# The closing of batch 6 on GpSimd, and the routed rows of batch 7 loaded from ScalarE's queue

## The reference

```python
x = x + ga * attention(h)                      # per batch
h = layernorm(x) * (1 + cb) + sb
topk_w, topk_i = group_limited_topk(softmax(h @ gate_weight.T))   # 2 of 8 experts per token
routed = sum over the 2 chosen experts of  w * (silu(h @ gate) * (h @ up)) @ down
shared = silu(h @ sh_gate.T) * (h @ sh_up.T) @ sh_down.T
x = x + gb * (routed + shared)                 # gb: one row of 256 per batch
```

## Time and profile before

| | |
|---|---|
| median of 3 runs | 278.69 us (278.34 to 280.42) |
| the profiled execution | 280.89 us, its span 278.9 us |
| mean granted clock of TensorE | 0.993 |
| busy: PE, DVE, ACT, POOL | 91%, 73%, 58%, 47% of the span |
| chain that ended last: PE, DVE, issue, ACT | 70%, 12%, 6%, 4% |

### The profile page before, as it was taken

The page is one execution under the profiler, slowest core; times in us unless marked ns, Lnnn a source line. Parts: engine busy times, 40 slices in busy tenths (PEclk is TensorE's granted clock), DMA queues, the critical chain, the costliest instruction groups (busy, mean ns, idle before and its releaser), DMA issues.

```text
span 278.9 us, 6194 instructions
## 1 busy us (share of the span) xinstructions
PE 254.6 (91%) x1797; PEld 235.3 (84%) x1797; DVE 202.8 (73%) x632; ACT 161.4 (58%) x429; POOL 132.1 (47%) x148
## 2 busy tenths in 40 slices
PE   0889999898999999999999889989999999999980
PEld 0787778797989999998979778989999999999960
DVE  1675974147998674388479778466899978989986
ACT  2447558968655754836536375355666666666630
POOL 4120313744255037785895375600455645555650
PEclk9999999999999999999999999999999999999997
DMA  7795007154224102242134023525754367485663
GB/s 230 272 346 160 0 7 228 49 158 125 74 66 127 47 1 98 95 124 86 67 119 139 34 84 123 202 81 130 199 151 129 123 205 235 135 239 211 227 190 118
DMA packets 28175, 37.89 MB, mean 136 GB/s; under 512 B 4476, under 2 KB 20711, under 8 KB 28144
## 3 DMA queue, kind: packets, MB, share of 16 engines
q1 hardware_dynamic: 23648, 28.63, 34.2%
q0 software_dynamic: 3216, 8.46, 8.1%
q10 hardware_dynamic: 1280, 0.41, 0.6%
HBM read 25.18 MB, written 12.71 MB: 136 GB/s over the span
## 4 chain that ended last, share of the span: by engine, by line
PE 70%; DVE 12%; issue 6%; ACT 4%; POOL 2%; DMA 2%; ACTq 1%; DVEq 0%; SPq 0%; POOLq 0%
PE bank L348 15%; PE bank L350 14%; PE bank L349 14%; PE bank L1148 4%; PE bank L1120 3%; PE bank L1367 3%; PE bank L1140 2%; PE bank L1103 2%; PE bank L1131 2%; PE bank L1112 2%; PE bank L1021 1%; PE bank L1398 1%; PE bank L1397 1%; DVE h2T_lo L1442 1%; DMA h2all<-routed_in 1%
## 5 line engine op out<-in xcount | busy, mean ns | idle before, releaser
L1496 POOL DMA_INDIRECT routed_out<-yo_all,dest x35 | 38.6, 1102 | 44.2 <-ACT yo_all L1438 32.1
L711 POOL DMA_INDIRECT routed_in<-h2all,slot_u x32 | 31.6, 986 | 21.8 <-DVE slot_u L692 11.6
L348 PE MATMUL bank<-experts_w,h2T_lo 128*128 x117 | 39.7, 339 | 0.1
L350 PE MATMUL bank<-experts_w,h2T_hi 128*128 x117 | 36.2, 309 | 0.0
L349 PE MATMUL bank<-experts_w,h2T_hi 128*128 x117 | 36.0, 307 | 0.0
L348 PE MATMUL bank<-h2T_hi,wsgu_lo 128*128 128x256 f32 (+1 forms) x96 | 27.9, 290 | 0.7 <-ACT og L482 0.7
L350 PE MATMUL bank<-h2T_hi,wsgu_hi 128*128 128x256 f32 (+1 forms) x96 | 27.0, 281 | 0.0
L349 PE MATMUL bank<-h2T_lo,wsgu_hi 128*128 128x256 f32 (+1 forms) x96 | 26.9, 281 | 0.0
L1422 ACT ACTIVATE wstage<-bank 128x176 f32<-128x176 f32 x39 | 12.4, 318 | 22.1 <-PE bank L350 22.1
L348 PEld LDWEIGHTS bank<-experts_w,h2T_lo 128*128 128x128 f32 x117 | 22.2, 190 | 0.8 <-issue 0.6
L349 PEld LDWEIGHTS bank<-experts_w,h2T_hi 128*128 128x128 f32 x117 | 22.3, 190 | 0.0
(11 more groups left out here) (278 smaller groups left out, 827.8 us busy)
## 6 DMA issues: line engine op xcount, KB each, us to landing
h2all<-routed_in SPq DMA_DIRECT2D x39, 130.0 KB, 2.5
wstage<-gu_t SPq DMA_DIRECT2D x8, 352.0 KB, 3.2
res<-x SPq DMA_DIRECT2D x4, 512.0 KB, 8.9
mx_all<-modrow SPq DMA_DIRECT2D x8, 256.0 KB, 3.2
mh_all<-modrow SPq DMA_DIRECT2D x8, 256.0 KB, 3.4
exchange<-routed_out SPq DMA_DIRECT2D x4, 512.0 KB, 4.8
wmod_s<-w_mod SPq DMA_DIRECT2D x3, 512.0 KB, 10.0
out<-res SPq DMA_DIRECT2D x6, 256.0 KB, 3.1
```

The costliest lines, as they stand in the source:

```text
L348: pe.matmul(out_ap, l[1], r[0], start=start, stop=False)
L350: return pe.matmul(out_ap, l[0], r[0], start=False, stop=stop)
L711: pool.indirect_dma_start(out=routed_in, out_offset=bass.IndirectOffsetOnAxis(slot_u[:, i, j:j + 1], 0), in_=h2all[:, j % (2 * NB), :], in ...
L1496: pool.indirect_dma_start(out=routed_out, out_offset=bass.IndirectOffsetOnAxis(dest[:, t % 16:t % 16 + 1], 0), in_=yo[t % 6], in_offset=No ...
```

## The change

Batch 6 joins batch 5 in BY_POOL: its three closing steps run on POOL behind those of batch 5, and not on DVE. FIN_AT gets a fifteenth number (37), so that batch 4 "out" is taken at tile step 37 of DVE. `load_rows` of batch 7 goes from SP, where it stood behind that of batch 6, to ACT, where it stands in tile step 37 between the copy L1426 of that tile and the copy out (L1434) of tile 36.

```diff
-            BY_POOL = (5,)
+            BY_POOL = (5, 6)
...
-                    for b in (6, 7):
-                        load_rows(sp, b)
+                    load_rows(sp, 6)
                     store(sp, 4)
                     store(sp, 6)
                     store_half(sp, 7, 0)
...
                         act_tile_act(act, t, r)
+                        if t == LASTT - 1:
+                            load_rows(act, B - 1)
...
-                    FIN_AT = (20, 21, 22, 23, 24, 25, 28, 29, 30, 31, 32, 33, 35, 36)
+                    FIN_AT = (20, 21, 22, 23, 24, 25, 28, 29, 30, 31, 32, 33, 35, 36, 37)
```

## The result

The changed kernel took 283.64 us in the median of 13 runs (280.76 to 285.14), the kernel before 280.42 in the median of 13 runs beside them (278.34 to 281.26). The ratio is 1.0107, with a 95% interval of 1.0075 to 1.0138: 3.0 us slower, between 2.1 and 3.9. The ratio leaves out one slow run of the changed kernel (285.14), so it isn't quite the quotient of the two medians. The 278.69 on which the forecast stands was the median of three runs, which are the first three of these thirteen of the kernel before. The forecast was +0.5 us and a range that ended at 280.4, 1.7 above that median; the time is outside, on the slow side, on either footing (280.42 + 1.7 is 282.1).

What follows compares the result with a forecast made beforehand. It took the end to be DVE's tail plus one small store: last store 277.05 + 1.8 landing + 0.2 for three close stores + 0.35 = 279.4, or +0.5 us; on the median 278.69 that gives 279.2 us, range 277.6 to 280.4.

Steps and rivals of the forecast that it cites:

- So the end is DVE's tail plus one small store.: At the kernel's end: last store at 276.75 plus 1.8 to land gives 278.55; the span ends 0.35 us later.
- the walk: Step-by-step times of POOL and DVE in the new tail: POOL ends at 275.95, DVE at 277.0.
- The rivals: Other tail outcomes: early rows 277.8 us (chance 0.17), no hold-up between engines 278.6 (0.13), late rows 280.3 (0.17).
- Batch 4 "out" ahead of a remainder: On DVE near 268.00, this 0.60 us operation delays the last remainder by 0.3 us, between 0 and 0.6.
- The load on ACT: In tile step 37, ACT issues batch 7's load at 266.14, before its next copy, at cost 0.
- The rows: Loads of batches 6 and 7 on two queues share the transfers; both land at 271.4.
- POOL and DVE block each other: In the tail, two-SBUF-input operations wait for each other: POOL's steps 1.3 to 1.8 us, some of DVE's 0.5 to 1.2 longer.
- The sum up to the last store: End of the tail: after DVE's last operation at 277.0, the last half store of batch 7 leaves at 277.05.
- the last store of batch 6 leaves behind 275.9: Sign to look for on the changed kernel's timeline: batch 6's last store is issued after 275.9.
- the transfers were not at their limit with 283 GB/s: On the two 512 KB row loads, the forecast took transfers as the limit: 283 GB/s, DMA engines 87% busy.

Runs made afterwards that it cites:

- e4: The kernel before with only batch 7's load moved from SP to ACT; batch 6 closed on DVE as before: 0.9994 of the kernel before.
- e3: The changed kernel with both loads kept on SP, so batch 6 still closes on POOL: 1.0078 of the kernel before.
- e1: The changed kernel with its last block closed without GpSimd's DRAIN: 1.0009 of the kernel before.
- e2: The kernel before with its block closed without GpSimd's DRAIN: 1.0029 of the kernel before.
- e7: The changed kernel with both loads kept on SP and the block closed without GpSimd's DRAIN: 0.9995 of the kernel before.

## Why the prediction was wrong

*The step that failed* stands in the first part: "So the end is DVE's tail plus one small store." I had 276.75 + 1.8 = 278.55 and passed over what the block's end consists of, since 0.35 us seemed too little to ask about. That 2.9 meets 3.0 so well is in part luck, for the walk had POOL's end 0.6 us too late: forecast 275.95, measured 272.90 + 1.26 + 1.16 = 275.32. In the absolute time (279.2 against 283.64) a further 1.7 us is the median of before itself, 278.69 in three runs and 280.42 in thirteen.

*The rivals* with a time all kept the same model of the end and so lay within 1.6 us of no change. That is why the range was too narrow: not the sizes were unsure, but a resource was missing.

*What held.* The terms of the walk, on the clock of before (the rows above plus 1.16):

- Batch 4 "out" ahead of a remainder, forecast 0.3 between 0 and 0.6: the last remainder starts 4.23 behind that of tile 35, before 3.94. It is 0.29.
- The load on ACT: forecast start 266.14 and no cost. 265.04 + 1.16 = 266.20, 0.43 long; ACT's next copy starts at 265.56 and had to wait for PE anyway. e4 confirms it with 0.9994.
- The rows, forecast 271.4 for both: DVE's and POOL's "sum" start with them, batch 6 at 269.81 + 1.16 = 270.97, batch 7 at 271.56. Batch 6's took 4.8 us from the issue (3.9 before), batch 7's 5.3 (5.1). Two loads on two queues share, and batch 6's loses 0.9 us of its precedence: from its issue to its landing it took 3.5 to 4.1 us in the traces with both loads on SP (4.0 in e3), 4.5 to 5.1 in those with one on ACT. That is what the rule quoted from the Trainium skill ("DMA: Bandwidth & Descriptors", "Queues, rings and completion order") gives; the traces agree.
- POOL and DVE block each other: forecast 1.3 to 1.8 for POOL's steps, 0.5 to 1.2 more for some of DVE's. POOL's were 1.27, 1.53, 1.26, so only the middle one was stretched; DVE "sum" 1.23 instead of 0.69, the two "scale" 2.04 instead of 0.75. "sum" ended 0.55 behind POOL's (269.81 + 1.27 = 271.08, 271.63), as in the earlier trace rows; "late", which reads PSUM, kept its 0.75. The Trainium skill states this as an exclusive lock ("SBUF — State Buffer", "SBUF: two separate sides"), for a DVE operation with two SBUF inputs against a GpSimd operation that reads SBUF; the trace agrees.
- The sum up to the last store was 0.7 us too high: forecast 277.05, measured 275.15 + 1.16 = 276.31, because the rows of batch 6 came 0.4 earlier and one hand-over between DVE and POOL fell away. Landing 2.0 instead of 1.8, as forecast. The sign "the last store of batch 6 leaves behind 275.9" failed with it: that store left at 274.19 + 1.16 = 275.35.
- One reading of rows was wrong without harm: the transfers were not at their limit with 283 GB/s. From 268 to 269 us 360 GB/s moved before, and 393 after the change, with the store of batch 4 among the loads.

Without the DRAIN the end would be at 276.31 + 2.0 + 0.35 = 278.66, -0.2 us; e1 measures 1.0009. So the change has next to nothing to gain even then: batch 7's "sum" begins with its rows, but POOL's steps, twice as long as DVE's, take turns with DVE's and hold up "sum" and "scale" by 1.8 us together (1.23 - 0.69 and 2.04 - 0.75).

## What to carry to other kernels

- GpSimd's DRAIN behind an ordinary operation took 0.082 us for each indirect DMA (128 rows of 1 KB) issued since its last DRAIN, and 0.1 more: 5.60 us for 67, 2.97 for 35, 2.7 for 32, 0.67 for 7; one that followed another with nothing between them took 0.04. Directly behind a scatter among the tiles it took more, 4.7 and 5.8 us for 28.
- The other engines' DRAINs took 0.007 us (SP), 0.15 (ACT), 0.58 (DVE) and 0.78 (PE), the last two with the end of the engine's last work in them.
- From the start of the last scatter to the moment when a wait for it is over, 2.4 us went by in eight of the thirteen traces and 3.2 to 4.0 in the other five. Between e2 and e7, with 4.0 us in both traces, only e7 had nothing else to do meanwhile, and its tail was 12.9 where e3's trace had let me expect 11.35. The cause of the spread stays open.
